# DMA transposes in place of TensorE transposes, a ring of three PSUM banks for maxima and sums, and six matmuls at the entry of a batch's heads

## The chip, the cores and the metric

The kernel runs on one core of a Trainium2 chip. The metric is the device time of one execution in microseconds (us), lower is better. Beside the five compute engines (TensorE, called PE in the profile; its weight loads, PEld; VectorE, DVE; ScalarE, ACT; GpSimd, POOL) there is SyncE (SP), which issues the DMAs. Line numbers (L1612) are those of the kernel before.

## The reference

A stack of two layers on 4 sequences of 1024 tokens, 256 channels. Layer 0 (a gated convolution, an MLP, a mixture of experts) isn't touched by the change. The change lies in layer 1, which for each sequence computes

```python
q, k, v = (heads(x @ w.T) for w in (w_q, w_k, w_v))       # 16 heads of 16 channels
q, k = rope(q), rope(k)
scores = where(block_causal_mask, q @ k.T / 4, -inf)       # 1024 x 1024 a head, about half is kept
ctx = softmax(scores) @ v @ w_o.T
h = sparsify_2to4(silu(x1 @ w_gate) * (x1 @ w_up))         # x1: layernorm(x + ctx)
out = layernorm(x1 + h @ w_down)
```

with a layernorm ahead of it too.

## The kernel before

Everything below is in `attention_ffn_phase`, which runs once, after layer 0 has left its result in SBUF. A loop over the four sequences ("batches", `b`) has two parts: `heads(b)`, then projection, layernorm and the feed-forward network of `b`. In the second part the rows of the next batch `c = b + 1` are made among the feed-forward work. Each engine has its instruction order written out by hand; semaphores tie them.

**Rows of q and k.** A batch has `ST` = 8 tiles of 128 tokens. For tile `t`, `x_high` (ACT) and `x_low` (DVE) split x into two f16 parts (`xs`, two buffers). `x_transposed` (TensorE, L1851) puts four 128x128 transposes into PSUM, `xt_copied` (ACT, L1381) copies them to `xt`, and `qkv` (TensorE, L1864) multiplies. `qkv_copied` (ACT, L1389 and L1392), `rotate` (DVE), `high_part` and `part_copies` (ACT), and `low_parts` (DVE) then write the rows of all heads into `qks`, 64 columns a head: three f16 parts, two columns for the negated row maximum, one for the mask.

**Turned rows.** 16 heads are four groups `g` of two pairs. `qk_transposed` turns one pair's rows of q or k with eight 128x128 transposes (L1870), and `qk_copied` (ACT, L1408, 128x1024 f16) copies them to `qT` or `kT`. `first_rows` does it for group 0 of the next batch inside the feed-forward part.

**Maxima.** For each pair 20 jobs `m`: `for_maximum` (TensorE, L1903, L1906) makes plain scores of 128 to 512 columns in one of the two banks of `X`, `maximum` (DVE, L1607 and L1612) reduces them. A job waits for the reduction of job m - 2. After 20 jobs `max_parts` (DVE, three short instructions, L1618 to L1628) writes the maxima into the q rows, and the q rows of the pair are turned and copied a second time (`q_max_transposed` L1870, `q_max_copied` L1412). Only then can the pair's real scores be made.

**Heads.** A group has 20 steps `s` (10 units of two pairs). A step is `scores` (TensorE, L1930, into one of the two banks of `W`), `exponentials` (ACT, L1418) and, at even steps, `weighted` (TensorE, L1950). `sums_copied` (ACT, L1424), `sums_transposed` (TensorE, L1959, always into the bank `C`) and `normalised` (DVE, L1641, L1645) follow twice a group. `C` also takes the turned rows of later groups. Among the steps of one group stand the maxima of the next: two jobs a step, six of group 1 before step 0 (`AHEAD = 6`):

```python
            def heads(b):
                scores(b, 0, 0)
                qk_transposed(b, 1, 0, 1)
                wait(pe, qm_ok, group(b, 0)(2, 1))
                qk_transposed(b, 1, 0, 0)
                for_maxima(b, 1, 0, AHEAD)
                q_max_transposed(b, 0, 1)
```

So 57 steps carry maxima and the last 23 steps of the 80 carry none. SP issues only loads and the stores of the output in this phase.

## Time and profile before

| | |
|---|---|
| median of 3 runs | 1810.37 us (1805.66 to 1812.74) |
| profiled execution | 1815.68 us, of which the traced span is 1813.9 us |
| busy in the span | PE 1541.0, DVE 1153.2, ACT 821.9, POOL 220.9 us |
| mean granted TensorE clock | 0.922 of 2.4 GHz |
| layer 1 | from about 685 us to the end |
| `heads` of the four batches | 121.8, 123.8, 122.5, 123.2 us |

The heads of a batch are counted here from the end of `max_parts` of group 0, pair 1 (786.5, 1052.2, 1316.7, 1585.8 us) to the first transpose of the finished context (908.3, 1176.0, 1439.2, 1709.0 us). In a timeline row a duration covers the whole run of "xN" like instructions, and the bracket says how long the engine was idle before the first and what ended that. Matmuls overlap: the distance between starts is the pace, not the duration.

### The profile page before, as it was taken

The numbers are of one execution on the slowest core, as the hardware profiler recorded it, in microseconds if no ns is written. First come the engines' busy times: TensorE is split into PE (matmuls) and PEld (weight loads), VectorE is DVE, ScalarE is ACT, GpSimd is POOL, SyncE is SP. The second block draws the span as 40 slices with busy tenths as digits, with TensorE's granted clock in tenths as the row PEclk, the third lists the DMA queues.
The fourth block names the chain that finished last, engine by engine and source line by source line (L and its number), as shares of the span: only waits on it lengthen the run. The fifth ranks groups of instructions, "written<-read, shape, count | busy, mean of one in ns | idle before, by whom it ended". The sixth has DMA issues, their size and how long they took to land.

```text
span 1813.9 us, 27446 instructions
## 1 busy us (share of the span) xinstructions
PE 1541.0 (85%) x10490; PEld 877.8 (48%) x10491; DVE 1153.2 (64%) x2401; ACT 821.9 (45%) x1352; POOL 220.9 (12%) x236
## 2 busy tenths in 40 slices
PE   4999999869989973689888989788989788889796
PEld 2666666545568871233354534255433344433345
DVE  5666677545420145678568678678778578778475
ACT  5445555313112213347854157753177663167530
POOL 2343444302410001000000000100000100000000
PEclk8999999879998986669999989999989999989999
DMA  2001010024124402000000000000000000000000
GB/s 107 13 24 36 23 31 27 12 80 117 39 64 141 132 1 96 1 1 1 1 1 1 0 1 1 25 1 1 1 1 1 25 1 0 1 1 2 24 1 24
DMA packets 27153, 48.04 MB, mean 26 GB/s; under 512 B 7312, under 2 KB 16016, under 8 KB 26256
## 3 DMA queue, kind: packets, MB, share of 16 engines
q1 hardware_dynamic: 26464, 44.74, 7.6%
q0 software_dynamic: 576, 1.77, 0.3%
q8 instruction: 74, 1.21, 0.3%
q14 instruction: 39, 0.32, 0.1%
HBM read 37.59 MB, written 9.06 MB: 26 GB/s over the span
## 4 chain that ended last, share of the span: by engine, by line
issue 60%; POOL 2%; DVE 0%; POOLq 0%; DVEq 0%
POOL rs_sb L1340 1%; POOL ve_sb L1337 0%; POOL qks_sb L1355 0%; POOL v_sb L1354 0%; POOL qks_sb L1345 0%; DVE bn_sb L1545 0%; DVE x_sb_sb L1560 0%; POOLq L1159 0%; POOLq L66 0%; POOL qks_sb L1356 0%; DVE mv_sb L1551 0%; DVEq L1159 0%; POOL v_sb L1353 0%; DVE ident_h_sb L1742 0%; DVEq L66 0%
## 5 line engine op out<-in xcount | busy, mean ns | idle before, releaser
L1612 DVE TENSOR_REDUCE mx_sb<-s_ps 128x1 f32<-128x512 f32 (+1 forms) x512 | 313.1, 652 | 116.1 <-PE s_ps L1906 67.8
L1418 ACT ACTIVATE room_sb<-s_ps 128x1024 f32<-128x1024 f32 (+1 forms) x320 | 283.2, 948 | 24.0 <-PE s_ps L1930 22.9
L1903 PE MATMUL s_ps<-room_sb 48*128 48x512 f16 (+3 forms) x640 | 177.2, 345 | 37.8 <-DVE mx_sb L1607 18.7
L1930 PE MATMUL s_ps<-room_sb 51*128 51x128 f16 (+4 forms) x1152 | 145.9, 283 | 22.7 <-ACT room_sb L1418 15.1
L1950 PE MATMUL cm_ps<-room_sb,v_sb 128*32 128x512 f32 (+3 forms) x1536 | 162.8, 513 | 0.8 <-ACT room_sb L1424 0.8
L1903 PEld LDWEIGHTS s_ps<-room_sb 48*128 48x128 f16 x640 | 52.8, 95 | 208.8 <-DVE mx_sb L1612 124.9
L2072 PE MATMUL cm_ps<-w_fd_sb,room_sb 128*128 128x256 f32 x512 | 132.3, 407 | 14.7 <-DVE room_sb L1694 14.7
L1337 POOL TENSOR_TENSOR ve_sb<-mv_sb,eps_sb 128x4 f32<-128x4 f32 x24 | 5.0, 210 | 1086.2 <-DVE mv_sb L1551 1086.2
L396 DVE SCALAR_TENSOR_TENSOR x_sb_sb<-xp_sb,conv_w_sb,x_sb_sb 128x512 f32<-128x512 f32 x96 | 106.6, 1113 | 22.6 <-ACT x_sb_sb L319 20.5
L2072 PEld LDWEIGHTS cm_ps<-w_fd_sb,room_sb 128*128 128x128 f32 x512 | 97.8, 199 | 38.9 <-issue 14.1
L2059 PE MATMUL s_ps<-xbT_sb,w_fg_sb 128*128 128x512 f16 x384 | 100.9, 393 | 10.3 <-DVE ctok_sb L1660 8.7
L2059 PE MATMUL s_ps<-xbT_sb,w_fu_sb 128*128 128x512 f16 x384 | 103.5, 401 | 0.0
L966 PE MATMUL em_ps<-xT_sb,ws_gu_sb 128*128 128x512 f32 x192 | 93.2, 632 | 7.9 <-DMA rows<-zeros 7.9
L1930 PEld LDWEIGHTS s_ps<-room_sb 50*128 50x128 f16 (+1 forms) x1152 | 54.7, 97 | 79.0 <-ACT room_sb L1418 49.9
L1906 PE MATMUL s_ps<-room_sb 51*128 51x128 f16 x512 | 83.4, 233 | 10.7 <-ACT room_sb L1408 10.0
L402 DVE SCALAR_TENSOR_TENSOR m1T_sb<-mm_ps,m1T_sb 128x512 f16<-128x512 f32 x64 | 44.0, 688 | 56.6 <-ACT m1T_sb L311 56.3
L1464 ACT ACTIVATE sgl_sb<-s_ps 128x512 f32<-128x512 f32 x64 | 37.9, 593 | 86.3 <-PE s_ps L2059 86.1
L1607 DVE TENSOR_REDUCE mx_sb<-s_ps 128x2 f32<-128x512 f32 (+1 forms) x128 | 66.0, 554 | 13.2 <-PE s_ps L1906 12.8
L490 PE MATMUL ro_ps<-w_dn_sb,m1T_sb 128*128 128x256 f16 x256 | 69.9, 273 | 0.8
L492 PE MATMUL ro_ps<-w_dn_sb,m1T_sb 128*128 128x256 f16 x256 | 69.8, 273 | 0.0
L491 PE MATMUL ro_ps<-w_dn_sb,m1T_sb 128*128 128x256 f16 x256 | 69.8, 273 | 0.0
L1851 PE MATMUL s_ps<-ident_h_sb,xs_sb 128*128 128x128 f16 x128 | 13.0, 227 | 61.1 <-DVE xs_sb L1575 39.1
(256 smaller groups left out, 3034.6 us busy)
## 6 DMA issues: line engine op xcount, KB each, us to landing
we_gu_sb<-we_gu SPq DMA_DIRECT2D x32, 352.0 KB
we_dn_sb<-we_dn SPq DMA_DIRECT2D x32, 176.0 KB
x_in_sb<-x SPq DMA_DIRECT2D x9, 512.0 KB, 3.5
rows<-x_sb_sb SPq DMA_DIRECT2D x8, 512.0 KB, 3.0
x_sb_sb<-rows SPq DMA_DIRECT2D x2, 2048.0 KB, 11.5
out<-x_sb_sb SPq DMA_DIRECT2D x8, 512.0 KB, 2.6
xp_sb<-w_in SPq DMA_DIRECT2D x1, 1024.0 KB, 7.9
x_sb_sb<-w_up SPq DMA_DIRECT2D x1, 1024.0 KB, 8.6
```

Of the source, the lines that this page charges most:

```text
L396: dve.scalar_tensor_tensor(xc[:, c, :], xp[:, c, k:k + GTOK], conv_w[:, c, k:k + 1], xc[:, c, :], ALU.mult, ALU.add)\
L490: pe.matmul(out, of[0][at], by[0][cols], start=start, stop=False)
L491: pe.matmul(out, of[1][at], by[0][cols], start=False, stop=False)
L966: last = pe.matmul(mm[c % 4][:, :], ws_gu[:, k, col:col + P], xT[:, k, g * GTOK:(g + 1) * GTOK], start=(k == 0), stop=(k == KD - 1))
L1418: act.activation(weights[(g * NU + u) % SLOTS_P][:, 2 * pair:2 * pair + 2, 0:width(u) * P], W[s % 2][:, :, 0:width(u) * P], ACT.Exp, scale ...
L1612: dve.tensor_reduce(mx[:, pair, k % 2, slot:slot + 1], X[:, k % 2, 0:count * P], AX.X, ALU.max, negate=True).then_inc(mx_ok, 1)
L1903: last = pe.matmul(X[:, k % 2, at * P:(at + plain) * P], query[head:head + NORM, i * P:(i + 1) * P], key[head:head + NORM, j * P:(j + plai ...
L1906: last = pe.matmul(X[:, k % 2, (at + plain) * P:(at + count) * P], query[head:head + USED, i * P:(i + 1) * P], key[head:head + USED, i * P ...
L1930: last = pe.matmul(W[s % 2][:, head, (at + low - i) * P:(at + high - i) * P], key[first:first + rows, j * P:(j + 1) * P], query[first:firs ...
L1950: last = pe.matmul(O[32 * h:32 * h + 32, (i - half * GT) * P:(i - half * GT + count) * P], v[:, j, g * HG + h, :], weights[(g * NU + u) % ...
L2059: last = pe.matmul(bank[:, e, :], wt[:, j, k, ch * P:(ch + 1) * P], xh[:, g, k, i, :], start=(k == n == 0), stop=(k == KD - 1 and n == 2))
L2072: last = pe.matmul(CM[:, t // 2, (t % 2) * D:(t % 2 + 1) * D], hs[:, k % 3 * 4 + i, t * P:(t + 1) * P], w_fd[:, k % 2 * 4 + i, :], start=( ...
```

## The change

1. **x and the rows of q and k are turned by DMA.** SP issues `dma_start_transpose`, SBUF to SBUF: one of 128x512 f16 per token tile (`x_turned`, 8 a batch), and for each group and pair one of 128x1024 f16 for k and one for q (`turned_rows`, 16 a batch), and one for q with its maxima (`q_max_turned`) in groups 1 to 3 (6 a batch). Group 0's second turn of q stays on TensorE and ACT. `x_transposed`, `xt_copied`, `qk_transposed`, `qk_copied` and `first_rows` are gone. `qks` is laid out anew so that a pair's rows are 1024 contiguous elements a partition, and the columns of `w_qk` are in another order.
2. **Three banks in turn** (`RING`: the two of `X`, and `C`) for the maxima of groups 1 to 3 and for `sums_transposed`. A job waits for the reader of the job three turns before. Group 0's maxima keep the two banks of `X`.
3. **`AHEAD = 8`, and no maxima before step 0.** Group 1's first 24 jobs stand three a step in steps 0 to 7 of group 0, then two a step; the last 24 steps carry none.
4. **Entry of the heads.** After the first `scores`, `kept_busy` issues six 128x128 by 128x512 f16 matmuls into a bank of `W`; nothing reads them. `q_max_copied` of pair 1 stands on ACT behind the first exponential.
5. Waits that go with it: the two constant loads `w_o` and `w_fd` count into `consts`, which DVE awaits before it writes the mask column. `qkv` waits for the landing of its x. `all_q_max_landed` holds the next batch's writes into `qks`.

```diff
-AHEAD = 6
+AHEAD = 8
+        RING = (X[:, 0, :], X[:, 1, :], C)
         def max_jobs(g, s):
-            return (g + 1, AHEAD + 2 * s) if AHEAD + 2 * s < 2 * NX else (g + 2, AHEAD + 2 * s - 2 * NX)
+            if g == 0 and s < AHEAD:
+                return ((1, 3 * s, 3 * s + 3),)
+            low = AHEAD + 2 * s
+            return ((g + 1, low, low + 2),) if low < 2 * NX else ((g + 2, low - 2 * NX, low - 2 * NX + 2),)
...
+        def ring_bank_read(b, turn):
+            if turn < 2:
+                return mx_ok, group(b, 0)(2 * NX, LEAD + 2 * NX - 1 + turn)
+            if turn == 2:
+                return f2_ok, 2 * b
+            kind, g, i = jobs[turn - 3]
+            if kind == "max":
+                return mx_ok, group(b, g)(2 * NX, LEAD + i + 1)
+            return cn_ok, group(b, g)(2, LEAD + i + 1)
...
+            def x_turned(c, t):
+                k = c * ST + t
+                wait(sync, xs_low, k + 1)
+                wait(sync, qkv_mm, k - 1)
+                sync.dma_start_transpose(xt[:, t % 2, :, :, :].rearrange("p a f c -> p (a f) c"),
+                                         xs[:, t % 2, :, :].rearrange("p a c -> p (a c)")).then_inc(xt_in[t % 2], 16)
+            def turned_rows(b, g, pair):
+                n = b * NHG + g
+                before = n - (3 if pair == 0 and g == 3 else 2)
+                if g == 0:
+                    wait(sync, sc_mm, STEPS * n)
+                elif g == 3 or (g, pair) == (2, 1):
+                    wait(sync, sc_mm, STEPS * (before + 1))
+                wait(sync, qk_in[pair], 32 * n)
+                for tiles, s in ((kT, 1), (qT, 0)):
+                    sync.dma_start_transpose(of_pair(tiles, g, pair).rearrange("p (t c) -> p t c", t=ST),
+                                             rows_of(g, s, pair)).then_inc(qk_in[pair], 16)
+            def q_max_turned(b, g, pair):
+                wait(sync, nm_ok, group(b, g)(2, LEAD + pair + 1))
+                q_max_landed(sync, b, g, pair, 1)
+                sync.dma_start_transpose(of_pair(qT, g, pair).rearrange("p (t c) -> p t c", t=ST),
+                                         rows_of(g, 0, pair)).then_inc(qmT, 16)
+            for b in range(NB):
+                for t in range(ST):
+                    x_turned(b, t)
+                wait(sync, ca_ok, (b + 1) * ST)
+                wait(sync, low_ok, (b + 1) * ST)
+                wait(sync, zeroed, b + 1)
...
+                for pair in range(2):
+                    turned_rows(b, 0, pair)
+                wait(sync, hs_ok, 4 * b)
+                turned_rows(b, 1, 0)
+                turned_rows(b, 1, 1)
+                turned_rows(b, 2, 0)
+                for g in range(1, NHG):
+                    q_max_turned(b, g, 0)
+                    q_max_turned(b, g, 1)
+                    if g == 1:
+                        turned_rows(b, 2, 1)
+                        turned_rows(b, 3, 0)
+                    if g == 2:
+                        turned_rows(b, 3, 1)
+                if b > 0:
+                    stored(b - 1)
...
             def for_maximum(b, g, m):
...
-                wait(pe, mx_ok, q(2 * NX, LEAD + m - 1))
+                if g == 0:
+                    wait(pe, mx_ok, q(2 * NX, LEAD + m - 1))
+                else:
+                    wait(pe, *ring_bank_read(b, turns["max", g, m]))
...
+            def kept_busy(bank, count):
+                for i in range(count):
+                    pe.matmul(bank, ident_h[:, :], w_qk[:, 0, 0, :], start=True, stop=True)
             def heads(b):
                 scores(b, 0, 0)
-                qk_transposed(b, 1, 0, 1)
-                wait(pe, qm_ok, group(b, 0)(2, 1))
-                qk_transposed(b, 1, 0, 0)
-                for_maxima(b, 1, 0, AHEAD)
-                q_max_transposed(b, 0, 1)
+                kept_busy(S[1][:, 0, :], 6)
+                q_max_transposed(b, 1)
...
-                        if g + 1 < NHG:
-                            if s == 3:
-                                if g > 0:
-                                    wait(pe, cn_ok, group(b, g - 1)(2, LEAD + 2))
-                                qk_transposed(b, g + 1, 1, 1)
...
-                if ahead:
-                    x_transposed(c, 0)
...
-                    if ahead and w in (NF, NF + 1):
-                        first_rows(c, w - NF)
```

## Rows read from the trace of the kernel before

**Rows 1.** Part 1 of the page: busy time, share of span, instructions.

```profile
PE 1541.0 (85%) x10490; PEld 877.8 (48%) x10491; DVE 1153.2 (64%) x2401; ACT 821.9 (45%) x1352; POOL 220.9 (12%) x236
```

**Rows 2.** Windows, stage by stage: the heads, and one feed-forward part.

```profile
core 0: us, PE busy (x) PEld busy (x) DVE busy (x) ACT busy (x) POOL busy (x), PEclk, DMA share, GB/s
...
786.50:908.30 121.80, 106.19 (x1064) 42.77 (x1062) 84.73 (x181) 93.96 (x111) 2.41 (x4) 0.94 0.00 1
...
1052.20:1176.00 123.80, 106.05 (x1056) 41.81 (x1056) 91.59 (x205) 93.29 (x111) 4.83 (x8) 0.94 0.03 10
1176.00:1316.70 140.70, 124.33 (x640) 69.74 (x640) 107.76 (x209) 49.82 (x98) 2.92 (x8) 0.96 0.00 1
1316.70:1439.20 122.50, 104.90 (x1056) 41.88 (x1056) 91.75 (x206) 93.31 (x111) 4.82 (x8) 0.96 0.03 10
...
1585.80:1709.00 123.20, 107.05 (x1053) 42.23 (x1053) 85.11 (x179) 92.20 (x108) 2.41 (x4) 0.93 0.03 10
```

**Rows 3.** Windows of shorter stretches; the columns are those of rows 2.

```profile
827.50:857.90 30.40, 28.29 (x298) 11.98 (x296) 25.40 (x51) 24.03 (x29) 0.00 (x0) 1.00 0.01 2
883.20:908.30 25.10, 20.19 (x220) 6.92 (x216) 8.80 (x32) 21.77 (x29) 2.41 (x4) 1.00 0.00 1
1055.00:1065.00 10.00, 7.51 (x57) 2.72 (x55) 5.95 (x11) 6.08 (x6) 0.00 (x0) 0.52 0.01 2
...
1220.00:1257.00 37.00, 30.75 (x176) 14.41 (x174) 33.62 (x64) 19.09 (x38) 0.00 (x0) 0.95 0.00 1
```

**Rows 4.** Window of DVE alone, first to last maximum of batch 0's groups 1 to 3.

```profile
core 0: us, DVE busy (x), PEclk, DMA share, GB/s
789.00:883.20 94.20, 75.89 (x148) 0.93 0.01 1
```

**Rows 5.** Timeline, two steps of a steady group (start, duration, engine, instruction).

```profile
846.23 2.48 DVE L1612 TENSOR_REDUCE mx_sb<-s_ps 128x1 f32<-128x512 f32 x4 [0.82 <-PE s_ps L1903]
...
846.35 0.62 PE L1870 MATMUL cm_ps<-ident_h_sb,qks_sb 128*128 128x128 f16 x8
...
847.01 1.02 ACT L1408 ACTIVATE room_sb<-cm_ps 128x1024 f16<-128x1024 f16 x1 [0.39 <-PE cm_ps L1870]
...
847.58 0.39 PE L1903 MATMUL s_ps<-room_sb 48*128 48x512 f16 x1 [0.21 <-DVE mx_sb L1612]
...
848.12 1.06 PE L1950 MATMUL cm_ps<-room_sb,v_sb 128*32 128x512 f32 x8
```

**Rows 6.** Timeline of DVE and ACT at the entry of batch 1's heads.

```profile
1060.13 3.77 ACT L1418 ACTIVATE room_sb<-s_ps 128x1024 f32<-128x1024 f32 x4
...
1062.28 1.29 DVE L1612 TENSOR_REDUCE mx_sb<-s_ps 128x1 f32<-128x512 f32 x2 [1.05 <-PE s_ps L1906]
1065.00 2.48 DVE L1612 TENSOR_REDUCE mx_sb<-s_ps 128x1 f32<-128x512 f32 x4 [1.43 <-PE s_ps L1903]
```

**Rows 7.** Timeline of PE in the first batch's q, k, v (702 to 753 us).

```profile
719.70 0.45 PE L1851 MATMUL s_ps<-ident_h_sb,xs_sb 128*128 128x128 f16 x4 [2.61 <-DVE xs_sb L1575]
719.94 2.77 PE L1864 MATMUL s_ps<-w_qk_sb,xt_sb 128*128 128x512 f16 x6
722.50 1.23 PE L1864 MATMUL s_ps<-w_v_sb,xt_sb 128*128 128x256 f16 x6
726.34 0.40 PE L1851 MATMUL s_ps<-ident_h_sb,xs_sb 128*128 128x128 f16 x4 [2.61 <-DVE xs_sb L1575]
```

**Rows 8.** Timeline of PE in the feed-forward part between batches 1 and 2.

```profile
1196.68 0.38 PE L1851 MATMUL s_ps<-ident_h_sb,xs_sb 128*128 128x128 f16 x4 [2.84 <-ACT v_sb L1392]
...
1241.40 1.42 PE L1870 MATMUL s_ps<-ident_h_sb,qks_sb 128*128 128x128 f16 x16
```

**Rows 9.** Waits in the same part: us in total, times, longest.

```profile
PE s_ps L1851 <- ACT v_sb L1392: 6.1, 5, 2.8
```

**Rows 10.** DMA issues: KB each, median us from issue to landing.

```profile
out<-x_sb_sb SPq DMA_DIRECT2D x8, 512.0 KB, 2.6
...
w_fd_sb<-w_fd SPq DMA_DIRECT2D x1, 1024.0 KB, 9.6
...
room_sb<-w_v SPq DMA_DIRECT2D x1, 256.0 KB, 4.4
...
w_o_sb<-w_o SPq DMA_DIRECT2D x1, 256.0 KB, 7.7
```

More of the change, by code:

```diff
@@ L1342, in zero_columns @@
             def zero_columns(c):
-                wait(pool, tm_mm, 2 * NHG * c)
-                for g in range(NHG):
-                    last = pool.memset(qks[:, :, g * 2 * HG:g * 2 * HG + HG, NORM:FILTER], 0.0)
-                last.then_inc(zeroed, 1)
+                all_q_max_landed(pool, c)
+                pool.memset(all_rows[:, 0, :, NORM:FILTER], 0.0).then_inc(zeroed, 1)
             pool.memset(power[:], -0.5)
@@ L1491, in _ @@
             part_copies(0, ST - 1)
-            for pair in range(2):
-                for s in (1, 0):
-                    qk_copied(0, 0, pair, s)
-            q_max_copied(0, 0, 0)
+            q_max_copied(0, 0)
             for b in range(NB):
@@ L1620, in max_parts @@
                 wait(dve, joined, q(2, pair + 1))
-                own = slice(g * 2 * HG + 2 * pair, g * 2 * HG + 2 * pair + 2)
-                parts = [qks[:, :, own, NORM + c] for c in range(2)]
+                parts = [qks[:, 0, 2 * g + pair, :, :, NORM + c] for c in range(2)]
                 least = mx[:, pair, :, 0:ST].rearrange("p h t -> p t h")
@@ L1718, in heads @@
             def heads(b):
-                maxima(b, 1, 0, AHEAD)
                 for g in range(NHG):
@@ L2088, in _ @@
             pe.wait_ge(ready, 2)
-            for pair in range(2):
-                first_rows(0, pair)
             for_maxima(0, 0, 0, NX + 4)
-            q_max_transposed(0, 0, 0)
+            q_max_transposed(0, 0)
             for_maxima(0, 0, NX + 4, 2 * NX)
```

269 lines of the change are left out of this document (104 added, 165 removed).

## The prediction

> **What bounds the kernel now.** I read part 1 of the page first: in the whole span PE is busy 85%, DVE 64% [rows 1]. Such shares mix stages, so next I cut layer 1 into windows, ending each heads part where the context transposes begin. The four heads parts take 121.8 + 123.8 + 122.5 + 123.2 = 491.3 us [rows 2]; in each all three engines are busy between 69 and 87%, so none is plainly the bound.
>
> Shorter windows separate it. A steady group takes 30.4 us, with DVE busy 25.4, PE 28.3 and ACT 24.0 [rows 3]. The timeline says why: DVE reduces four maxima in 2.48 us, then stands 0.82 us waiting for PE, a period of about 3.3 us [rows 5]. PE may run only two jobs ahead. It makes its last maximum when DVE has freed a bank (847.58, after a wait), then in order does a `scores` and the `weighted` at 848.12 (pace about 1 us), and by then DVE has eaten both banks. So the loop PE -> DVE -> PE through two banks sets the pace. The eight transposes (0.62 us) fill time in which PE would have waited for that bank anyway; the 1.02 us copy on ACT lies beside DVE too. From first to last maximum of groups 1 to 3 DVE works 75.9 of 94.2 us [rows 4]; idle is 18.3. Behind it is a tail without maxima of 25.1 us, where ACT is busy 21.8: ACT bounds it [rows 3]. At the entry the order is turn, copy, turn, copy, then the first exponential: it starts at 1060.1, 8 us after the maxima of group 0 ended at 1052.2; DVE gets one job at a time (waits 1.05, 1.43), and TensorE's granted clock is 0.52, its lower level, from 1055 to 1065 [rows 3, 6].
>
> Outside the heads two stretches matter. In the first batch's q, k, v the period of a token tile is 726.34 - 719.70 = 6.6 us: transposes, `qkv` at mostly the lower clock, copies and parts on ACT and DVE, and only then the next `x_low`, for which PE waits 2.61 us [rows 7]. In the feed-forward part (140.7 us, PE busy 124.3 [rows 2]) PE waits 6.1 us before transposes of x, because their bank is half of the one that `qkv_copied` reads [rows 8, 9]; later DVE is busy 33.6 of 37 us [rows 3].
>
> **The change part by part.** I make the sum against the profiled execution (1815.7 us).
>
> *The third bank.* PE can now fill three banks before it turns to `scores` and `weighted`, so DVE holds one more reduction, 2.48 / 4 = 0.62 us, against an idle time of 0.82: 0.2 us are left per two steps [rows 5]. Maxima stand in 56 steps, so 28 x 0.2 = 5.6 us idle beside 75.9 us of work: 81.5 instead of 94.2. Bounds: 75.9 (idle gone) and 94.2 (PE, with 28.3 of 30.4 busy, keeps the pace itself; transposes are only some 6 x 0.6 = 3.6 of it).
>
> *Entry, AHEAD = 8.* No copy stands before the first exponential any more, and DVE starts on group 1 as soon as PE has turned pair 1's q. Now first maxima start at 789.0, 2.5 us after the previous ones ended [rows 2, 4]; I take 1.3. Its main gain, the 1 us waits at the lower clock, is in the 94.2 already.
>
> *Tail.* 24 steps instead of 23: 25.1 x 24 / 23 = 26.2 [rows 3].
>
> *The six matmuls.* Six times 512 columns. A 512-column f16 matmul had a pace of 0.43 us at the lower clock (six in about 2.6 us [rows 7]), so 1.3 us at full clock and 2.6 at half. They stand where PE waits for the last reductions of group 0, with `max_parts`, so I cost them at nothing; uncovered they cost 1.3 to 2.6 us a batch. Whether they keep the clock up I can't read; for lower-clock stretches that stay I put down 1.5 us a batch, between 0 and 4.
>
> *The transposes by DMA.* No row shows one. Plain transfers of 256 KB, the size of one 128x1024 f16, landed in 4.4 and 7.7 us, 512 KB stores in 2.6, 1024 KB in 9.6 [rows 10]. I take L = 4.4 us, the row of the same size with least queued before it, and keep 2.6 and 9.6 as ends. Almost all have cover: group 1's turned rows are issued when the feed-forward's last hidden rows are done, (2,1) and (3,0) some 7 steps before their first maximum. Late next is `q_max_turned` of pair 1: its maxima end at step 15, and PE needs it at step 0 of the next group, behind 8 jobs of the group after. DVE needs for the seven of them that gate PE about 3.4 us (an estimate: 0.62 for 512 columns, less for the narrower ones, [rows 5]). So L - 3.4 = 1.0 us of PE, with `weighted` and the maxima queued behind it, in two groups; in the last one no maxima follow and four steps hide it. 2.0 us a batch.
>
> A page of the Trainium skill speaks against this part: VectorE: DVE Perf Modes, "The three transpose paths", gives 1309 ns for a 128x128 through the DMA against 390 ns on TensorE, and advises TensorE where PSUM will do. By it (an estimate) eight blocks one after the other are 10.5 us; in the trace eight TensorE transposes take 0.62 us, and no run yet shows the DMA's. DMA: Bandwidth & Descriptors, "Latency and other measured facts", gives 261 GB/s for such transposes, which with the 2 us of fixed cost that the page also gives would be 3.0 us. By the first the sum below turns into the slow rival, by the second the 2.0 us vanish.
>
> *Heads in sum:* 1.3 + 81.5 + 26.2 + 2.0 + 1.5 = 112.5 us; four times 450.0 against 491.3: **-41 us**.
>
> *First batch's rows.* Without a transpose on PE the x of tile t + 2 is no longer behind `qkv` of t + 1: the same loop, 6.4 us plus L, now serves two tiles, (6.4 + 4.4) / 2 = 5.4 instead of 6.6 us [rows 7]. Six tiles: -7.4, and +3.4 for the first landing: **-4**. With L = 2.6 it is -11, with 7.7 about +9. The wait for `w_fd` costs nothing: it is issued some 4 us after the phase's start at 685, lands in 9.6 [rows 10], and DVE needs it at 702.
>
> *Feed-forward, three times.* Gone from PE: 6.1 us of waits [rows 9], eight times four x transposes (about 0.2 us pace each set, 1.8), and 32 row transposes (about 1.3 and 0.9, 2.2); from ACT the copies. The sum is 10, but DVE is busy 33.6 of 37 us soon after [rows 3], which returns a good half: 4.5 us each, **-13**. Bounds 0 and 10 each.
>
> *DVE and POOL edits* (memsets, one mask write instead of eight, strides of `qks`) keep the element counts: nothing.
>
> Sum: 1815.7 - 41 - 4 - 13 = 1757.7 profiled. The median of the runs lies 5.3 us under the profiled time: 1752.
>
> **The rivals.**
> 1. *PE is the bound.* The steady group has PE at 28.3 of 30.4 us [rows 3]. If the work left, about 25 us with its semaphore gaps, sets 29.5 a group, the third bank brings little: 3 x 0.9, entry 3 and the like, 6 us a batch: 1815.7 - 24 - 4 - 3 = 1785, median about 1780. For it: that share. Against: PE's own waits for DVE in the same cycle [rows 5].
> 2. *Landing takes 7.7 us* [rows 10]. The two groups stall 4.3 each, the third 2.7: 11.3 a batch instead of 2.0, +37; the first batch +13. 1752 + 50 = 1802. Against: that row had over 2 MB queued before it.
> 3. *The other side: transposes pass one after the other and slowly.* Twelve are due inside the heads (six with maxima, six turned rows). Once one takes more than 110 / 12 = 9.2 us they set the heads, whatever the banks do; the stalls alone, 2(L - 3.4) + (L - 5) a batch against 66 us of gains without them, cross zero at L = 9.4 too. At 10.5 us the heads take 126 us and what waits behind, about 130: +7 x 4 on the kernel before, the first batch's tiles (6.4 + 10.5) / 2 = 8.4, +11 and +9 for the first landing, and the feed-forward's gain is lost to late x: 1810 + 28 + 20, about 1858. Against: 256 KB in 9.6 us would be four times slower than any plain row [rows 10]. The page above gives 10.5.
> 4. *Better than forecast:* L = 2.6 and all DVE idle gone: 22 + 8 (stalls) + 7 (first batch) less than the forecast, about 1715.
>
> **How the numbers follow.** Forecast 0.53 (own range 1732 to 1770), rival 1 0.16, rival 2 0.08, rival 3 0.17, rival 4 0.06. The range from 1725 to 1812 leaves out rival 3 and part of rival 4, about 2 in 10. A change under 0.5% (9 us) is about what this kernel's runs can't tell from none. Rival 2 lies half within it: same 0.06. Faster: 0.53 + 0.16 + 0.06 + half of rival 2 = 0.78; slower, the rest, 0.16.
>
> **What would show it.** In the profile of the changed kernel: DVE's idle before L1612's counterpart falls from 0.8 to some 0.2 us per four reductions, and a steady group takes about 28 us; the heads last 110 to 114 us; the first exponential begins before the last copy of q; no 0.5 clock for 10 us at the entry; q, k, v of the first batch has a period near 5.4 us; SP's transposes land in 3 to 5 us, and PE's longest waits in the heads are for the landing of q with maxima, 1 us. The prediction falls if transposes take over 9 us or delay one another, if PE is busy all through a group at 29 us or more, or if the feed-forward part grows because the landing of x is late.

## The result, and the profile after

| | before | after |
|---|---|---|
| median | 1808.01 us (4 runs, 1804.88 to 1812.74) | 1751.20 us (4 runs, 1749.66 to 1755.88) |
| profiled execution (its span) | 1815.68 us (1813.9) | 1749.66 us (1747.8) |
| mean granted clock | 0.922 | 0.917 |

The ratio is 0.9695, with a 95% interval of 0.967 to 0.9721: faster by 3%, and 1 us from the forecast of 1752. That closeness is partly luck, as the sum by stages below shows. Part 1 of the page after, beside [rows 1]:

```profile
PE 1479.3 (85%) x9682; PEld 826.3 (47%) x9683; DVE 1146.7 (66%) x2395; ACT 732.6 (42%) x1232; POOL 219.9 (13%) x225
```

Windows after, cut as in [rows 2]: the first batch's rows, then heads and feed-forward parts in turn.

```profile
core 0: us, PE busy (x) PEld busy (x) DVE busy (x) ACT busy (x) POOL busy (x), PEclk, DMA share, GB/s
677.80:768.32 90.52, 46.53 (x183) 17.57 (x184) 67.58 (x133) 25.79 (x54) 7.91 (x12) 0.61 0.35 89
768.32:880.74 112.42, 97.24 (x929) 35.03 (x927) 82.92 (x181) 78.34 (x92) 2.41 (x4) 0.92 0.18 29
...
1024.19:1135.02 110.83, 94.18 (x926) 34.14 (x925) 90.16 (x205) 77.08 (x90) 4.82 (x8) 0.94 0.20 39
1135.02:1279.85 144.83, 125.29 (x570) 67.41 (x570) 107.92 (x209) 43.64 (x87) 2.83 (x5) 0.93 0.14 26
1279.85:1389.23 109.38, 92.78 (x926) 33.81 (x925) 90.07 (x206) 77.08 (x90) 4.82 (x8) 0.95 0.19 40
...
1533.74:1643.45 109.71, 94.06 (x926) 34.37 (x925) 83.33 (x180) 76.37 (x88) 2.41 (x4) 0.94 0.18 39
```

With the same cuts in both traces, the difference of the two profiled spans, 66.1 us, adds up like this:

| | before | after | change | forecast |
|---|---|---|---|---|
| layer 0 (code unchanged) | 684.9 | 677.8 | -7.1 | 0 |
| first batch's rows and first maxima | 101.7 | 90.5 | -11.2 | -4 |
| four heads parts | 491.4 | 442.3 | -49.1 | -41 |
| three feed-forward parts | 431.1 | 432.8 | +1.7 | -13 |
| last tail | 104.9 | 104.3 | -0.6 | 0 |

The total hides errors of opposite sign: 15 us more than forecast gained in the heads and the first batch's rows, and 15 us not gained in the feed-forward parts. Layer 0 lies between 675.1 and 684.9 us in the profiles of all these kernels, so its 7 us are scatter between executions, and most of what the profiled times differ by beyond the medians (66 against 57).

Windows of the first heads part after, from the first to the last maximum of groups 1 to 3, and the tail behind it ([rows 4], and the second row of [rows 3]):

```profile
770.82:855.67 84.85, 75.01 (x700) 27.11 (x697) 73.53 (x145) 55.55 (x63) 0.00 (x0) 0.90 0.22 35
855.67:880.74 25.07, 19.73 (x217) 6.54 (x213) 9.38 (x36) 21.20 (x28) 2.41 (x4) 1.00 0.06 12
```

The maxima took 94.2 us and now take 84.9; the forecast was 81.5, with 1.5 us for the lower clock put down beside it. A steady group, beside the first row of [rows 3], and the pattern that the timeline of VectorE repeats near its end:

```profile
826.00:853.00 27.00, 23.57 (x253) 9.22 (x253) 24.95 (x52) 19.41 (x22) 0.00 (x0) 1.00 0.22 40
```

```profile
852.29 1.28 DVE L1674 TENSOR_REDUCE mx_sb<-s_ps 128x1 f32<-128x512 f32 x2
853.49 0.68 DVE L1674 TENSOR_REDUCE mx_sb<-cm_ps 128x1 f32<-128x512 f32 x1
854.39 1.29 DVE L1674 TENSOR_REDUCE mx_sb<-s_ps 128x1 f32<-128x512 f32 x2 [0.23 <-PE s_ps L1938]
```

`cm_ps` is the third bank. The idle time before a burst fell from 0.82 [rows 5] to 0.2 us, as forecast, and a group takes 27.0 us instead of 30.4. The DMA issues after (KB aren't given for transposes):

```profile
room_sb<-qks_sb SPq DMA_TRANSPOSE x88, 3.3
...
xt_sb<-xs_sb SPq DMA_TRANSPOSE x32, 2.5
```

The number behind a kind of DMA is the median of its times from issue to landing. A 128x1024 transpose landed in 3.3 us, where I had taken 4.4.

### The profile page after: what moved, and what is told of

The parts are those of the page before. It is cut to its first block, busy times and chain, and to the rows that moved or that the text cites. A ratio compares the mean times of both kernels' runs of the same rounds, so it can differ in the third digit from the quotient of the medians.

```text
span 1747.8 us, 25797 instructions
## 1 busy us (share of the span) xinstructions
PE 1479.3 (85%) x9682; PEld 826.3 (47%) x9683; DVE 1146.7 (66%) x2395; ACT 732.6 (42%) x1232; POOL 219.9 (13%) x225
## 4 chain that ended last, share of the span: by engine, by line
issue 59%; POOL 2%; DVE 0%; POOLq 0%; DVEq 0%
POOL rs_sb L1443 1%; POOL ve_sb L1440 0%; POOL qks_sb L1457 0%; POOL v_sb L1455 0%; DVE bn_sb L1607 0%; DVE x_sb_sb L1622 0%; POOLq L1159 0%; POOLq L66 0%; POOL qks_sb L1447 0%; DVE mv_sb L1613 0%; DVEq L1159 0%; POOL v_sb L1454 0%; POOL qks_sb L1458 0%; DVE ident_h_sb L1803 0%; DVEq L66 0%
## 5 line engine op out<-in xcount | busy, mean ns | idle before, releaser
L1509 ACT ACTIVATE room_sb<-s_ps 128x1024 f32<-128x1024 f32 (+1 forms) x320 | 291.2, 941 | 167.1 <-PE s_ps L1965 162.5
L1674 DVE TENSOR_REDUCE mx_sb<-s_ps 128x1 f32<-128x512 f32 (+1 forms) x400 | 249.4, 649 | 63.5 <-PE s_ps L1941 40.2
L1938 PE MATMUL s_ps<-room_sb 48*128 48x512 f16 (+3 forms) x480 | 152.3, 354 | 30.6 <-DVE mx_sb L1669 16.3
L1965 PE MATMUL s_ps<-room_sb 51*128 51x128 f16 (+4 forms) x1152 | 150.4, 283 | 15.4 <-ACT room_sb L1509 10.6
L2067 PE MATMUL s_ps<-xbT_sb,w_fg_sb 128*128 128x512 f16 x384 | 107.3, 412 | 14.3 <-DVE ctok_sb L1722 12.7
L1938 PEld LDWEIGHTS s_ps<-room_sb 48*128 48x128 f16 x480 | 42.5, 95 | 161.7 <-DVE mx_sb L1674 85.0
L1910 PE MATMUL s_ps<-w_qk_sb,xt_sb 128*128 128x512 f16 x192 | 51.3, 406 | 49.2 <-DMA xt_sb<-xs_sb 31.4
L1965 PEld LDWEIGHTS s_ps<-room_sb 50*128 50x128 f16 (+1 forms) x1152 | 58.5, 97 | 65.8 <-ACT room_sb L1509 44.9
L1941 PE MATMUL s_ps<-room_sb 51*128 51x128 f16 x360 | 69.7, 238 | 19.6 <-DMA room_sb<-qks_sb 12.0
L1674 DVE TENSOR_REDUCE mx_sb<-cm_ps 128x1 f32<-128x512 f32 (+1 forms) x112 | 73.3, 655 | 18.2 <-PE s_ps L1941 13.9
```

Of the source, the lines that this page charges most:

```text
L1509: act.activation(weights[(g * NU + u) % SLOTS_P][:, 2 * pair:2 * pair + 2, 0:width(u) * P], W[s % 2][:, :, 0:width(u) * P], ACT.Exp, scale ...
L1674: dve.tensor_reduce(mx[:, pair, k % 2, slot:slot + 1], max_bank(g, m)[:, 0:count * P], AX.X, ALU.max, negate=True).then_inc(mx_ok, 1)
L1938: last = pe.matmul(bank[:, at * P:(at + plain) * P], query[head:head + NORM, i * P:(i + 1) * P], key[head:head + NORM, j * P:(j + plain) * ...
L1965: last = pe.matmul(W[s % 2][:, head, (at + low - i) * P:(at + high - i) * P], key[first:first + rows, j * P:(j + 1) * P], query[first:firs ...
L2067: last = pe.matmul(bank[:, e, :], wt[:, j, k, ch * P:(ch + 1) * P], xh[:, g, k, i, :], start=(k == n == 0), stop=(k == KD - 1 and n == 2))
```

## The experiments

Each kernel is the changed one with one edit, unless said. The medians of runs 1 to 12 are over 5 to 12 executions each; the windows, of one profiled execution, are cut as above. That execution is the fastest of its kernel for the changed one (1749.66 us) and for run 7, and the slowest for run 1.

| kernel | median us | heads, sum | clock in them | feed-forward, sum | clock in them |
|---|---|---|---|---|---|
| before | 1808.0 | 491.4 | 0.93 to 0.96 | 431.1 | 0.93 to 0.96 |
| after | 1751.2 | 442.3 | 0.92 to 0.95 | 432.8 | 0.91 to 0.93 |
| 1 no six matmuls | 1756.4 | 448.9 | 0.89 to 0.91 | 433.3 | 0.92 to 0.93 |
| 2 two banks | 1835.5 | 519.9 | 0.74 to 0.92 | 439.3 | 0.90 to 0.94 |
| 3 two banks, old entry | 1807.2 | 499.0 | 0.85 to 0.93 | 434.3 | 0.91 to 0.92 |
| 4 x on TensorE | 1766.8 | 445.9 | 0.87 to 0.95 | 437.7 | 0.91 to 0.93 |
| 5 two banks, filled | 1818.4 | 508.2 | 0.88 to 0.92 | 434.2 | 0.91 to 0.94 |
| 6 three banks, old entry | 1760.5 | 452.8 | 0.87 to 0.94 | 429.4 | 0.92 to 0.93 |
| 7 first steps filled | 1744.6 | 435.8 | 0.97 to 1.00 | 434.1 | 0.90 to 0.95 |
| 8 x_high early | 1751.3 | 445.5 | 0.90 to 0.94 | 430.1 | 0.91 to 0.94 |
| 9 feed-forward filled | 1751.1 | 442.3 | 0.92 to 0.95 | 429.1 | 0.95 to 0.98 |
| 10 = 7 + 8 + 9 | 1748.7 | 438.8 | 0.97 to 0.99 | 436.4 | 0.91 to 0.95 |
| 11 q with maxima twice | 1803.3 | 499.7 | 0.80 to 0.86 | 428.5 | 0.91 to 0.94 |
| 12 half of the comparisons | 1723.9 | 441.1 | 0.93 to 0.95 | 403.0 | 0.93 to 1.00 |

How far a sum moves by itself can be read from the kernels that leave the stage's code alone. The heads' code is that of the changed kernel in runs 4, 8, 9 and 12: their sums, with the changed kernel's, lie between 441.1 and 445.9 us. The feed-forward code is unchanged in runs 1, 2, 3, 5, 6, 7 and 11: their sums lie between 428.5 and 439.3. A difference inside these bounds shows nothing by itself.

### 1. Without the six matmuls

```diff
                 scores(b, 0, 0)
-                kept_busy(S[1][:, 0, :], 6)
                 q_max_transposed(b, 1)
```

> The changed kernel without the six matmuls at the entry of a batch's heads; nothing reads their results, so all that is computed stays. Theory: they keep nothing up. In the changed kernel the granted clock falls to its lower level anyway, only some 15 to 19 us after the start of the heads instead of 13 to 15, and they stand where PE waits for the last reductions. Then the time stays within 4 us of the changed kernel's 1751. Rival: they hold the higher clock over the entry; without them each batch's heads have a lower-clock stretch at the very start, and lose 1.5 to 4 us each, so 6 to 16 us in all (1757 to 1767).

Measured 1756.41 us (1749.9 to 1758.84), ratio to the kernel before 0.9694 (0.9671 to 0.9718). The medians, 5 us apart, don't separate, since the ranges overlap. The expectation had put the theory within 4 us and the rival from 6 us on; 5 lies between. In the traces the heads' sum grew by 6.6 us, to 3 us above the bounds of unchanged heads. The start of batch 1's heads: first the changed kernel, in windows of 5 us for engine PE alone, then the kernel without the six, all engines:

```profile
1024.19:1029.19 5.00, 4.01 (x51) 1.00 0.00 0
1029.19:1034.19 5.00, 4.13 (x41) 0.88 0.01 3
1034.19:1039.19 5.00, 4.92 (x32) 0.50 0.00 0
1039.19:1044.19 5.00, 4.90 (x30) 0.50 0.29 54
1044.19:1049.19 5.00, 4.65 (x32) 0.76 0.00 2
```

```profile
1024.04:1026.00 1.96, 1.61 (x20) 1.07 (x21) 1.93 (x5) 1.02 (x1) 0.00 (x0) 0.74 0.00 0
1026.00:1047.00 21.00, 20.63 (x126) 7.00 (x122) 14.89 (x29) 9.73 (x11) 0.00 (x0) 0.50 0.07 14
```

The column ahead of the DMA share is the granted clock; 0.50 is its lower level, 1.2 GHz. Without the six, TensorE runs at it for 24 us, from 1 us after the entry (the second row holds 21 of them); with them it holds 2.4 GHz for 9 us and then has 14 us at the lower one. They delay and shorten the stretch and don't remove it. My theory that they hold nothing falls, by the stretches. They are worth 1.6 us a batch in these two traces; the medians don't show it clear of the scatter.

### 2, 3 and 6. Two banks or three, old entry or new

```diff
         def max_bank(g, m):
-            return X[:, m % 2, :] if g == 0 else RING[turns["max", g, m] % 3]
+            return X[:, m % 2, :]
         def sum_bank(g, half):
-            return RING[turns["sum", g, half] % 3]
+            return C
...
             def for_maximum(b, g, m):
...
-                if g == 0:
-                    wait(pe, mx_ok, q(2 * NX, LEAD + m - 1))
-                else:
-                    wait(pe, *ring_bank_read(b, turns["max", g, m]))
+                wait(pe, mx_ok, q(2 * NX, LEAD + m - 1))
...
```

The waits of `sums_transposed` go back to those for `C` as well.

> The changed kernel, with the maxima of groups 1 to 3 back in the two banks of X (a job waits for the reduction of job m - 2) and the sums back in C; DMA transposes, AHEAD = 8 and the entry stay. Theory: the third bank is what took DVE's idle time from 0.82 to 0.2 us per four reductions; the steady group goes back from 27 to about 30 us, 28 x 0.6 = 17 us less what PE gains by having no transposes, so 2 to 3 us a group, 8 to 10 us a batch, 30 to 40 us in all: 1781 to 1791. Rival: with the transposes gone from PE it is fast enough for two banks too; a group stays at 27 to 28 us and the whole grows by at most 10 us, to 1761.

Run 3 adds the old entry:

```diff
-AHEAD = 8
+AHEAD = 6
-            if g == 0 and s < AHEAD:
-                return ((1, 3 * s, 3 * s + 3),)
...
                 scores(b, 0, 0)
-                kept_busy(S[1][:, 0, :], 6)
+                for_maxima(b, 1, 0, AHEAD)
                 q_max_transposed(b, 1)
...
```

The copy of pair 1's q stands before the first exponential again, too.

> As the run with two banks, and the entry of the kernel before as well: AHEAD = 6, six maxima of group 1 before step 0, no six matmuls, the copy of pair 1's q before the first exponential. Of the change only the DMA transposes are left. Theory: the new entry is worth the first exponential's 3 to 5 us a batch, so this run is 8 to 16 us above the one with two banks, and it stands about 10 to 15 us under the kernel before: 1793 to 1800 (the first batch's rows give 11 of them). Rival: the entry is worth nothing, since DVE's chain of maxima bounds the heads anyway: equal to the run with two banks within 4 us.

Run 6 has that entry with three banks.

> The changed kernel, three banks kept, with the entry of the kernel before: AHEAD = 6, six maxima of group 1 before step 0, none of the six matmuls, the copy of pair 1's q before the first exponential. Theory: the third bank carries the heads' gain; the entry is worth what the later start of the exponentials shows, 3 us a batch, and what the six matmuls were worth (5 us in all): 1763 to 1770. Rival 1: as with two banks, where the old entry was 28 us faster, it is the better one here too: under 1745. Rival 2: the entry is worth 5 us or more a batch: above 1771.

Measured, in the order 2, 3, 6: 1835.52 us (ratio 1.0168, 1.0131 to 1.0205), 1807.24 (0.9987, 0.9968 to 1.0006) and 1760.54 (0.9752, 0.9729 to 0.9775). Run 3 was expected 8 to 16 us above run 2 and came out 28 below it, so neither its theory nor its rival holds. Run 6 came out 2 us under the 1763 to 1770 of its theory and far from both rivals. With two banks VectorE's idle time is what it was before, though TensorE now has no transposes between:

```profile
1396.60 2.48 DVE L1674 TENSOR_REDUCE mx_sb<-s_ps 128x1 f32<-128x512 f32 x4 [0.82 <-PE s_ps L1935]
```

So the two-bank loop was the limit, as the prediction read it in [rows 5]. But two banks cost 84 us in run 2, where I expected 30 to 40. Windows of the third batch's heads in it:

```profile
1321.00:1326.00 5.00, 3.60 (x45) 2.07 (x45) 4.83 (x10) 3.07 (x3) 0.00 (x0) 1.00 0.00 0
1326.00:1390.00 64.00, 57.50 (x347) 16.43 (x342) 37.66 (x73) 26.86 (x30) 0.00 (x0) 0.50 0.16 30
1390.00:1461.26 71.26, 57.49 (x540) 19.41 (x538) 49.82 (x125) 48.03 (x57) 4.82 (x8) 0.93 0.14 34
```

For 64 us on end TensorE was granted 1.2 GHz; matmuls take about twice as long there (the rows of section 9 show both), and VectorE was busy 38 of the 64 us. TensorE had been busy 3.6 of 5 us before it fell, waiting for the two banks in steps that now hold three jobs. The parts of the change are therefore not to be priced one by one: with two banks the new entry costs 28 us (1807 to 1835), with three it gains 9 (1761 to 1751). Run 3 has of the whole change only the DMA transposes, and is no faster than the kernel before: -11 in the first batch's rows, +8 in the heads, +3 in the feed-forward (the last inside the scatter). With them in place and the old entry, the third bank alone gives 46.2 us in the heads (499.0 to 452.8).

### 5. Two banks, with matmuls where the transposes had been

```diff
+            def filled():
+                for t in range(ST):
+                    pe.matmul(C[:, t % 4 * P:(t % 4 + 1) * P], ident_h[:, :], w_qk[:, 0, 0, 0:P], start=True, stop=True)
...
+                        if g + 1 < NHG:
+                            if s == 3:
...
+                                filled()
+                            if s == 5:
+                                filled()
...
```

> The run with two banks, and in the heads eight 128x128 f16 matmuls with unread results (into C) at each of 15 places where the kernel before had TensorE transposes of rows. Theory (the granted clock): with two banks the heads took 520 us because TensorE, relieved of its transposes but still stopped by the two banks, stood idle more often and was granted the lower clock for up to 65 us on end (mean granted clock 0.74 to 0.92 in the heads, 0.93 to 0.96 in the kernel before). Unread matmuls in the same places give back the activity: granted clock at least 0.92 in the heads, these at most 495 us, the whole at most 1810. Rival: the 520 us come from the order of the maxima (AHEAD = 8, three jobs a step) that two banks can't keep up with; more work on TensorE then only adds: 1835 or more, and the clock as low as before.

The kernel has 16 such places a batch, not the 15 of the expectation. Measured 1818.42 us, ratio 1.0067 (1.0046 to 1.0089): 17 us less than run 2 for more work on TensorE. The windows of its second and third heads part:

```profile
1036.42:1164.00 127.58, 108.73 (x1054) 42.42 (x1053) 92.18 (x205) 77.83 (x90) 4.82 (x8) 0.91 0.19 34
1309.98:1437.32 127.34, 108.61 (x1054) 42.54 (x1053) 92.08 (x206) 77.86 (x90) 4.82 (x8) 0.90 0.18 34
```

That adding work made it faster shows the clock as a cause. But the heads took 508 us, not 495, and the clock rose to 0.88 to 0.92 only. Run 3, with the old order, no fill and a clock no higher on average (0.85 to 0.93), had heads of 499. So the order of the jobs with two banks seems to cost too; no run separates it further.

### 7. Sixteen more unread matmuls in the first steps

```diff
             def scores(b, g, s):
                 wait(pe, exp_ok, q(STEPS, LEAD + s - 1))
+                if g == 0 and 1 <= s <= AHEAD:
+                    kept_busy(W[s % 2][:, 0, :], 2)
```

> The changed kernel with two more unread 128x512 matmuls ahead of the scores of each of steps 1 to 8 of group 0 (16 more a batch, into the half bank that those scores then overwrite). Theory (the granted clock): the lower-clock stretch of some 14 us that the changed kernel has from 9 us after the start of each heads part goes or gets shorter; at full clock the 16 matmuls cost 3.5 us of PE that DVE's reductions mostly cover, and the stretch costs 3 to 4 us: 1740 to 1748. Rival: the stretch comes anyway, and the matmuls add up to 0.44 us a step at the lower clock, on the path: 1755 to 1775.

Measured 1744.57 us (1740.03 to 1745.06), ratio 0.965 (0.963 to 0.9669), the fastest here that computes everything. The first 25 us of batch 1's heads, beside the rows of run 1:

```profile
1016.07:1041.07 25.00, 23.10 (x198) 7.95 (x197) 21.41 (x41) 14.00 (x16) 0.00 (x0) 1.00 0.06 12
```

The stretch is gone: 2.4 GHz over the 25 us, with 198 matmuls, 16 of them unread. The heads gained 6.5 us in sum, 1.6 a batch, net of the unread matmuls, and the medians differ by 6.6. So getting rid of 14 us at half the clock gave back little more than a tenth of their length. My reading is that TensorE doesn't set the pace in most of these steps; VectorE is busy 21.4 of the 25 us. The intervals of this run and of the changed kernel (from 0.967) lie just apart, and its slowest execution is faster than the fastest of the changed kernel (1749.66).

### 4. x turned by TensorE again

```diff
+            def x_transposed(c, t):
...
+                for a in range(2):
+                    for f in range(KD):
+                        at = (a * KD + f) * P
+                        last = pe.transpose(x_bank(c)[:, at:at + P], xs[:, t % 2, a, f * P:(f + 1) * P], ident_h[:, :])
+                last.then_inc(tx, 1)
...
-                for t in range(ST):
-                    x_turned(b, t)
```

> The changed kernel with x turned by TensorE and copied by ACT again, as in the kernel before, in all four batches; the rows of q and k are still turned by DMA. Theory: the first batch's rows lose what the change gave them, 11 us (period of a token tile 6.6 instead of 4.2 us), and the three feed-forward parts stay where they are (within 1.5 us each), because a loop between DVE and ACT bounds them at 5.3 us a tile with or without these transposes: 1759 to 1765. Rival: the feed-forward parts did gain from it, and lost the gain to something else (the landing of x, or the turned rows of group 0): then they change by 3 to 5 us each and the sum is above 1770, or, if the landing costs more than the transposes, below 1758.

Measured 1766.83 us (1759.57 to 1770.7), ratio 0.9754 (0.973 to 0.9779). The first batch's rows took 100.8 us instead of 90.5, and the feed-forward parts 437.7 instead of 432.8, 1.6 each, which is inside the scatter. The median lies 2 us above the range of the theory and under that of the rival. Of the first batch's gain of 11, ten come from x by DMA.

### 8. x_high earlier in the feed-forward

In both kernels VectorE takes one x tile in the feed-forward every 5.31 us, and waits 1.43 us for `x_high`. After:

```profile
1164.58 0.42 DVE L1638 TENSOR_TENSOR xs_sb<-x_sb_sb,xs_sb 128x256 f16<-128x256 f32 x1 [1.43 <-ACT xs_sb L1478]
...
1169.88 0.43 DVE L1638 TENSOR_TENSOR xs_sb<-x_sb_sb,xs_sb 128x256 f16<-128x256 f32 x1 [1.43 <-ACT xs_sb L1478]
```

```diff
                     silu(b, w)
+                    if ahead and w + 4 < ST:
+                        x_high(c, w + 4)
...
                         qkv_copied(c, w + 2)
-                    if ahead and w + 4 < ST:
-                        x_high(c, w + 4)
```

> The changed kernel with one ACT instruction moved: in the feed-forward part x_high of tile w + 4 stands right behind silu of w instead of last in the iteration. Nothing else. Theory: a loop between DVE and ACT (rotate, high_part, part_copies, magnitude, qkv_copied, x_high, x_low, rotate), with no TensorE transpose in it, sets the 5.31 us a tile that both kernels show, with DVE waiting 1.43 us for x_high each time; this is why the feed-forward parts did not get faster. Out of the loop, the tile takes 4.7 to 4.9 us, four to six tiles gain 0.4 us or more each, so 2 to 3 us a part, 6 to 9 us in all: 1742 to 1746. Rival: TensorE's own work (about 4.7 us a tile, more at the lower clock) or the later chain of maxima sets the parts' end: no change, within 3 us of 1751.

Measured 1751.26 us, ratio 0.9688 (0.9668 to 0.9708): no change. The loop was read rightly, since the wait is gone and the tiles came at 4.67 and 5.20 us:

```profile
1165.23 0.42 DVE L1638 TENSOR_TENSOR xs_sb<-x_sb_sb,xs_sb 128x256 f16<-128x256 f32 x1
...
1169.90 0.42 DVE L1638 TENSOR_TENSOR xs_sb<-x_sb_sb,xs_sb 128x256 f16<-128x256 f32 x1
...
1175.10 0.42 DVE L1638 TENSOR_TENSOR xs_sb<-x_sb_sb,xs_sb 128x256 f16<-128x256 f32 x1
```

But the three parts got only 2.7 us shorter together, inside the scatter. So this loop isn't what sets their length, and the theory falls as far as the parts go.

### 9 and 10. The feed-forward parts filled, and all together

In the changed kernel, TensorE's timeline in the second feed-forward part shows two waits of over 3 us for VectorE; the first stands just ahead of the place of the removed transposes ([rows 8], L1870). In the kernel before they were 2.9 and 1.6 us.

```profile
1197.46 2.72 PE L2067 MATMUL s_ps<-xbT_sb,w_fg_sb 128*128 128x512 f16 x6 [3.58 <-DVE ctok_sb L1722]
...
1201.39 1.46 PE L2067 MATMUL s_ps<-xbT_sb,w_fg_sb 128*128 128x512 f16 x6
...
1209.77 0.23 PE L1938 MATMUL s_ps<-room_sb 48*128 48x128 f16 x1 [3.04 <-DVE mx_sb L1669]
...
1211.72 1.46 PE L2067 MATMUL s_ps<-xbT_sb,w_fg_sb 128*128 128x512 f16 x3
```

The last row's three matmuls of 512 columns take 1.46 us, as long as six in the second row at 2.4 GHz: behind the 3.04 us wait TensorE runs at 1.2 GHz.

```diff
+                    if ahead and (w, i) == (10, 2):
+                        wait(pe, hm_ok, 16 * b + 10)
+                        kept_busy(S[1][:, 0, :], 10)
...
+                    if ahead and w in (NF, NF + 1):
+                        wait(pe, qkv_ok, (c + 1) * ST)
+                        kept_busy(X[:, 0, :], 4)
```

> The changed kernel with unread 128x512 matmuls in the feed-forward part, three times: four behind each of hidden 8 and 9 (where the kernel before turned the rows of the next batch's group 0) and ten where TensorE waits 3 us for DVE within hidden 10. Theory (the granted clock): without the transposes TensorE stands idle in a stretch that DVE bounds (1196 to 1210 us), is then granted the lower clock for 10 to 17 us, and so gives back what the transposes had cost; this is where the forecast 13 us of the feed-forward parts went. With the fill the clock there is at least 0.95 over the part, the three parts take at most 426 us instead of 433, and the whole 1741 to 1747. Rival: DVE's chain sets the end of the part, whatever the clock: parts within 3 us of 433 in sum, whole 1749 to 1755.

> All that seemed to help at once: the changed kernel with the unread matmuls in steps 1 to 8 of group 0, those in the feed-forward part, and x_high moved forward. Theory: the heads keep their 436 us, and the feed-forward parts, at nearly full clock, now show the earlier x_high too: 425 us or less; the whole 1732 to 1738. Rival: the parts trade clock for clock, a stretch cured in one place comes back in another, and the sum stays at 1742 to 1748.

Measured 1751.12 us (ratio 0.9704, 0.9682 to 0.9726) and 1748.69 (0.9675, 0.9651 to 0.9699). In run 9 the clock came back (0.98, 0.95, 0.95) and the parts took 429.1 us, 1.2 less each, which is inside the scatter (run 6 has 429.4 without any fill): the rival, that VectorE's chain sets the end whatever the clock, holds. In run 10 the clock in the same parts was 0.95, 0.91, 0.91 with the same matmuls in them, and they took 436.4. Which it is, the fills of the heads or the earlier `x_high`, these runs don't say. Run 10 is not better than run 7, and above the ranges of its theory and, by 1 us, of its rival.

### 12. Half of VectorE's comparisons

```diff
-                dve.tensor_tensor(ge[:, 0:3, :], row(0, 3), own[:, 1:4, :], ALU.is_ge)
+                dve.tensor_tensor(ge[:, 0:3, 0:256], row(0, 3), own[:, 1:4, 0:256], ALU.is_ge)
```

and so in each instruction of `compare` and `count`; `nb` is set to zero once at the start. The choice for the other 256 columns is left out, so the output isn't that of the reference.

> The changed kernel in which compare and count of the feed-forward part (VectorE, the choice of the two largest of four) do only the first 256 of 512 columns; the choice for the other columns is left out, so this is no version to use. It takes VectorE about 3 us of its 6.4 us in each of the four groups of a part, some 12 us of the 108 us in which it is busy there, and nothing from TensorE or ACT. Theory: VectorE's own chain (hidden, compare, count, keep_largest, with q and k of the next batch and the maxima between them) sets the length of the feed-forward parts, which is why 10 us less work on TensorE and ACT bought nothing, and full clock in them 1 us: then each part gets at least 6 us shorter, the three 415 us or less in sum instead of 433, the last part some 4 us or more, and the whole at most 1730. Rival: TensorE, busy 125 of 144 us there, sets the length: parts within 2 us each, whole 1743 or more.

Measured 1723.90 us (1716.58 to 1725.04), ratio 0.9526 (0.95 to 0.9551). Its three parts; beside the second stands the row 1135.02:1279.85 of after:

```profile
880.98:1011.86 130.88, 116.77 (x570) 63.79 (x570) 97.14 (x209) 43.49 (x87) 2.83 (x5) 1.00 0.15 29
1122.78:1257.01 134.23, 121.48 (x570) 66.14 (x570) 97.34 (x209) 43.67 (x87) 2.83 (x5) 0.96 0.15 28
1366.38:1504.27 137.89, 125.29 (x570) 69.04 (x570) 97.24 (x209) 43.75 (x87) 2.83 (x5) 0.93 0.16 27
```

VectorE is busy 10.6 to 10.7 us less in each, and the parts are 12.6, 10.6 and 6.6 us shorter, 29.8 together, with TensorE's instructions the same. That is far outside the scatter, and the theory holds: VectorE's work is on the path that sets the length of the feed-forward parts. In the first part the clock is 1.00, too; how much of its 12.6 us came from that isn't shown.

### 11. A later landing of q with its maxima

```diff
                 q_max_landed(sync, b, g, pair, 1)
-                sync.dma_start_transpose(of_pair(qT, g, pair).rearrange("p (t c) -> p t c", t=ST),
-                                         rows_of(g, 0, pair)).then_inc(qmT, 16)
+                for again in range(2):
+                    if again:
+                        wait(sync, qmT, 32 * (2 * (b * (NHG - 1) + g - 1) + pair) + 16)
+                    sync.dma_start_transpose(of_pair(qT, g, pair).rearrange("p (t c) -> p t c", t=ST),
+                                             rows_of(g, 0, pair)).then_inc(qmT, 16)
```

The counts that wait for this landing are doubled.

> The changed kernel with each q_max_turned done twice, the second time after the first has landed, to the same place, so the turned q with its maxima is ready some 3.3 us later. Theory of the prediction (3.4 us of cover for pair 1): at a landing of 6.6 us it gives stalls of 2 x 3.2 + 1.6 = 8 us a batch, 32 in all: 1775 to 1790. Rival: cover is longer than that, since TensorE has other work before the first scores that need it; then it costs under 3 us a batch: 1751 to 1762.

Measured 1803.27 us (1800.18 to 1810.97), ratio 0.9988 (0.9973 to 1.0003): nearly the whole gain of the change is lost, and more than theory and rival expected. The wait row of TensorE for this landing, over the whole trace (us in all, times, longest), after and here, and the window of this kernel's second heads part:

```profile
PE s_ps L1965 <- DMA room_sb<-qks_sb: 2.9, 4, 0.8
```

```profile
PE s_ps L1968 <- DMA room_sb<-qks_sb: 34.0, 12, 3.8
```

```profile
1036.39:1165.11 128.72, 107.86 (x926) 37.10 (x925) 90.63 (x205) 77.72 (x90) 4.82 (x8) 0.80 0.23 46
```

The prediction's arithmetic gives 2 x 3.2 + 1.6 = 8 us a batch, 32 in all, for a landing of 6.6 us, and the waits are 34.0. The total fits by luck, for the single waits don't: by the arithmetic the first two of a batch are 3.2 us and the last 1.6, and in the three later batches they are 2.1 to 2.2, 2.1 and 3.8. TensorE had the q again 6.2 to 6.5 us after the end of `max_parts`. So the cover is about 4.2 us in the first two groups and 2.4 in the last (estimates: 6.4 - 2.2 and 6.2 - 3.8).

The waits grew by 31.1 us, but the heads grew by 57.4. The clock around the second wait of this part, which ends at 1107.37 (TensorE alone):

```profile
1103.00:1109.00 6.00, 3.87 (x55) 1.00 0.74 136
1109.00:1126.00 17.00, 16.46 (x102) 0.50 0.19 36
1126.00:1136.00 10.00, 8.71 (x86) 0.99 0.01 2
```

Behind each of the twelve waits the granted clock fell from 2.4 to 1.2 GHz like this, here for 17 us, elsewhere for 3 us and more, which makes 0.80 to 0.86 over the heads. The waits themselves are little more than half of the price; that the rest is the lower clock is the reading that fits, and no run separates it. The Trainium skill (TensorE: Matmul & The Clock Gate, "HAM oscillation") describes this coupling of a DMA wait to the lower clock; the rows above agree.

## Why the prediction was right, and where it was not

**The third bank** was the right mechanism at about the right size: 84.9 us of maxima instead of 94.2 in the first batch (forecast 81.5), idle 0.2 us per burst. VectorE still stands idle 11.3 us of the 84.9, where 5.6 were forecast. Part of the 3.4 us missed is the stretch at the lower clock in that window (0.90): in run 7, with a clock of 0.97, this heads part is 2.2 us shorter; the forecast had 1.5 us for it in a term of its own. Runs 3 and 6 show the bank's gain alone, 46 us; rival 1, TensorE as the bound, is out: a steady group takes 27.0 us, where that case had 29.5.

**Entry and tail.** The first maximum starts 2.5 us after the previous ended in batch 0, against the 1.3 that I took; the tail takes 25.1 instead of 26.2. Together they are right, by luck. The heads came to 112.4, 110.8, 109.4 and 109.7 us, against 112.5.

**The stalls** (2.0 us a batch) were mis-sized: TensorE waited 2.9 us in all four batches together, 0.7 to 0.8 in each. This term makes 5 of the 8 us by which the heads beat the forecast. L was too long, 3.3 us and not 4.4, and the cover was wrong in both places. In the first two groups nothing waited, and by run 11 some 4.2 us are covered there, not 3.4. All four waits stand in the last group, where I had put none below L = 5: its cover is 2.4 us, since TensorE had the q after 3.1 us and waited 0.7. The consequence in the rivals is wrong too: at L = 7.7 I put 1802, and run 11 shows 1803 already at about 6.3, the lower clock coming with the waits.

**The transposes by DMA**, rival 3. They landed in 3.3 us, a third of the 9.2 at which it would have decided. My argument against it was wrong as written: 256 KB in 9.6 us is not four times slower than any plain row, since `w_o`, also 256 KB, took 7.7 [rows 10]. The Trainium skill's 1309 ns a block (VectorE: DVE Perf Modes, "The three transpose paths"), taken eight times in a row, gave an estimate of 10.5, and the trace disagrees; no run shows one block alone. Its other figure (DMA: Bandwidth & Descriptors, "Latency and other measured facts"), with the fixed cost, gave an estimate of 3.0, and the trace nearly agrees.

**First batch's rows.** -11.2 against -4. The period fell from 6.6 to some 4.2 us, not 5.4: `rotate` starts at 702.22, 706.61 and 710.60.

```profile
702.22 0.69 DVE L1646 TENSOR_TENSOR ro_sb<-qk_sb,cos_sb 128x512 f32<-128x512 f32 x1 [4.01 <-ACT v_sb L1488]
...
706.61 0.68 DVE L1646 TENSOR_TENSOR ro_sb<-qk_sb,cos_sb 128x512 f32<-128x512 f32 x1
...
710.60 0.68 DVE L1646 TENSOR_TENSOR ro_sb<-qk_sb,cos_sb 128x512 f32<-128x512 f32 x1
```

The landing of x took 2.5 us, near the lower end that I had kept, for which the prediction gives -11. Again the mechanism held and L was too long; the 6.4 us of the loop stand on no row, and with 2.5 they give a period of 4.45, near the 4.2. Run 4 confirms it: with x turned on TensorE again, 10.3 of the 11.2 us are lost.

**The feed-forward parts: the step that failed.** I put down 4.5 us each for the work taken off TensorE and ACT, "a good half" of 10, and they came out 0.6 longer each, which is no change within the scatter. I had the row against it in hand: VectorE busy 33.6 of 37 us [rows 3]. I charged it as a discount where it was a verdict. The step that failed is that half of what was taken off TensorE and ACT would shorten the part. Runs 9 and 12 show it from both sides: at nearly full clock the parts gain nothing beyond the scatter, and with 10.6 us off VectorE they gain 9.9 on average. TensorE's 6.1 us of waits [rows 9] moved from the transposes of x to `qkv`, in the same part:

```profile
PE s_ps L1910 <- ACT v_sb L1488: 6.3, 4, 3.0
```

and its two waits for VectorE in section 9 grew from 2.9 and 1.6 us to 3.6 and 3.0.

**The six matmuls and the clock.** They were free, as taken, and shorten the lower-clock stretch; 1.5 us a batch for what stays is near what run 7 gave back, 1.6 net. One sign that I expected failed: no 0.5 clock for 10 us at the entry. Some 14 us of it are still there, from 9 us after the entry on.

**Luck in the total.** Without the profiled layer 0's 7 us, the forecast's -58 stands against -59. That agreement is luck: the heads gained 8 us and the first batch's rows 7 us more than forecast, and the feed-forward parts 15 us less. (The chances of "faster" add up to 0.79, where I wrote 0.78.)

## What to carry to other kernels

A loop of two engines through two banks can be read from one idle time that recurs between an engine's bursts (0.82 us here), and a third bank is worth up to one more job of cover per burst (it was 46 us of 499 here). Ask of every stretch separately which engine is busy nine tenths of it: work taken off any other buys nothing there, and may return as waits. On TensorE a wait costs more than its length when the granted clock falls behind it, so the parts of such a change should be measured together and not only one by one, and unread matmuls where TensorE has gaps can pay (16 a batch gave 1.6 us a batch here). A sum that fits can hide parts that don't: compare each single term and each single wait.
